# A language-model tower on one core: attention features in 32-row groups, expert loads issued by ScalarE, constants by VectorE, and new orders

## The reference

```python
h = table[x]
h = h + attn0(layernorm(h))        # A: causal linear attention, elu features, 16 heads of 16
h = h + ffn0(layernorm(h))         # A: one 256x256 product, scaled rows
h = h + attn1(layernorm(h))        # B and C: softmax-kernel attention, 64 features a head,
                                   #   its own two layernorms, an FFN 256 -> 1024 -> 256
h = h + moe(layernorm(h))          # C: router, shared expert; then 8 experts, one for each token
# inside attn1, for q and for k:
xp = einsum('bhnd,md->bhnm', x * norm, proj)                        # 16 channels -> 64 features
diag = sum(square(x)) * 0.5 * norm * norm
out = ratio * (exp(xp - diag - stab) + EPS_K)    # stab: max over m for q, over n and m for k
```

## Time and profile before

| | |
|---|---|
| median of 3 runs | 720.42 us (719.12 to 721.68) |
| the profiled execution, its own time | 719.09 us |
| its span, first to last instruction | 717.3 us |
| TensorE busy | 666.2 us (93%) |
| VectorE busy | 488.2 us (68%) |
| ScalarE, GpSimd busy | 282.2 and 272.2 us (39%, 38%) |
| mean granted TensorE clock | 0.979 |

### The profile page before, as it was taken

One profiled execution on the slowest core, in us unless ns is written; L12 is line 12 of the kernel. 1 busy time (PEld: TensorE's weight loads), 2 busy tenths in 40 slices (PEclk: granted clock), 3 DMA queues, 4 the chain that ended last, 5 costly groups with the idle time before them and its releaser, 6 DMA issues.

```text
span 717.3 us, 15031 instructions
## 1 busy us (share of the span) xinstructions
PE 666.2 (93%) x5626; PEld 545.7 (76%) x5627; DVE 488.2 (68%) x1116; ACT 282.2 (39%) x664; POOL 272.2 (38%) x422
## 2 busy tenths in 40 slices
PE   3879899999999999999999999999938699999996
PEld 3667688888898898989888898899937365565654
DVE  1888999999889888888878977867525122323231
ACT  2345456546454462636355263454201032322221
POOL 6244344525426153342504325314201344454542
PEclk9999999999999999999999999999979799999998
DMA  7940000000011010000000000000063411012110
GB/s 266 417 181 9 2 10 8 9 9 9 8 17 16 17 9 16 1 16 9 9 16 1 17 8 9 17 16 8 9 191 117 119 38 48 27 41 66 54 54 11
DMA packets 17296, 34.18 MB, mean 48 GB/s; under 512 B 7617, under 2 KB 12240, under 8 KB 15952
## 3 DMA queue, kind: packets, MB, share of 16 engines
q1 hardware_dynamic: 12640, 24.89, 10.0%
q0 software_dynamic: 4592, 8.41, 4.7%
HBM read 28.74 MB, written 7.29 MB: 50 GB/s over the span
## 4 chain that ended last, share of the span: by engine, by line
PE 79%; DVE 7%; DMA 4%; issue 4%; POOL 3%; ACT 2%; SPq 0%; POOLq 0%; DVEq 0%; ACTq 0%
PE ps L1070 74%; PE ps L1075 2%; DMA x_rows<-send_x 2%; PE ps L1240 2%; DMA sorted_ids<-tokens,slot_u 1%; DVE S_sb L770 1%; DVE stats L711 1%; ACT qkA L687 1%; POOL rstd L412 1%; ACT yTB L677 1%; POOL H L380 1%; POOL preC L471 0%; DMA yA<-x_rows,ids 0%; POOL sorted_ids L483 0%; DVE yA L716 0%
## 5 line engine op out<-in xcount | busy, mean ns | idle before, releaser
L411 POOL TENSOR_TENSOR var_eps<-mv,ln_eps 128x1 f32<-128x1 f32 x112 | 27.7, 248 | 270.3 <-DVE mv L712 269.6
L1070 PE MATMUL ps<-yTC,we 128*128 128x128 f32 x1024 | 125.3, 277 | 0.5 <-DVE yTA L798 0.5
L1070 PEld LDWEIGHTS ps<-yTC,we 128*128 128x128 f32 x1024 | 120.5, 194 | 1.4 <-issue 1.0
L1070 PE MATMUL ps<-we,yTA 128*128 128x256 f32 (+1 forms) x288 | 96.9, 469 | 3.1 <-issue 1.5
L1070 PEld LDWEIGHTS ps<-we,yTA 128*128 128x128 f32 x288 | 54.3, 199 | 27.7 <-issue 22.1
L1070 PE MATMUL ps<-we,yTB 128*128 128x256 f32 (+1 forms) x216 | 71.8, 466 | 0.0
L412 POOL TENSOR_TENSOR rstd<-var_eps,pow_half 128x1 f32<-128x1 f32 x112 | 64.4, 575 | 8.8
L1070 PE MATMUL ps<-we,ffT 128*128 128x256 f32 x256 | 62.0, 385 | 0.0
L1070 PEld LDWEIGHTS ps<-we,yTB 128*128 128x128 f32 x216 | 40.3, 190 | 23.8 <-issue 21.0
L1070 PEld LDWEIGHTS ps<-we,ffT 128*128 128x128 f32 x256 | 46.2, 190 | 8.2 <-issue 3.2
L770 DVE TENSOR_TENSOR S_sb<-ps,causal_sb 128x512 f32<-128x512 f32 x64 | 40.5, 678 | 8.1 <-PE ps L1070 8.1
(11 more groups left out here) (183 smaller groups left out, 1329.1 us busy)
## 6 DMA issues: line engine op xcount, KB each, us to landing
we<-w_experts SPq DMA_DIRECT2D x7, 1536.0 KB, 15.3
we<-w_ff SPq DMA_DIRECT2D x2, 1024.0 KB, 8.4
x_rows<-send_x SPq DMA_DIRECT2D x16, 128.0 KB, 1.7
home_rows<-send_home SPq DMA_DIRECT2D x16, 128.0 KB, 1.7
rows_sb<-rows SPq DMA_DIRECT2D x1, 1664.0 KB, 6.3
we<-w_experts SPq DMA_DIRECT2D x3, 512.0 KB, 3.9
we<-w_qk SPq DMA_DIRECT2D x2, 512.0 KB, 3.7
we<-w_v SPq DMA_DIRECT2D x2, 256.0 KB, 4.0
```

The costliest lines, as they stand in the source:

```text
L411: link(pool.tensor_tensor(var_eps[:, k:k + 1], mv[:, k, 1:2], ln_eps[:], ALU.add))
L1070: return pe.matmul(o, a, b, start=start, stop=stop)
```

## The change

1. **Features in 32-row groups.** `proj_sb` shrinks to blocks of 32 rows (2 heads, 128 columns). One stage `b_kq` replaces `b_k` and `b_q`: 16 matmuls of 128 columns, in turn on the four row groups, each to a PSUM bank of its own. k and q then lie side by side in four banks; ACT copies k out in two instructions, and DVE's `b_qs` reads q in two halves, after ACT's copies (it now waits for `xk_read`).
2. **`a_den`**: eight matmuls of 256 columns in place of 16 of 128.
3. **The late expert loads** stand in ScalarE's table and are issued on its queue. SP keeps `x_out`, `home_out` and the id loads.
4. **The constants** are set by VectorE, before its first statistics.
5. **48 products of a constant** (`ones_sb` by itself, 16 bit) stand first on TensorE.
6. **New orders and lags on all five engines, new PSUM banks** and so new `after(...)` waits.

```diff
-        proj_sb = sb("proj_sb", [P, 4 * M])
+        proj_sb = sb("proj_sb", [P, 2 * M])
...
-            def features(banks, first_chunk):
+            def features(at, first_chunk):
                 for c in range(KD):
-                    for g in range(2):
-                        rows_of = slice(64 * g, 64 * g + 64)
-                        ins = matmul(banks[:, g, c * 4 * M:(c + 1) * 4 * M],
+                    for g in range(4):
+                        rows_of = slice(32 * g, 32 * g + 32)
+                        ins = matmul((xka, xkb)[g // 2][:, g % 2, at + c * P:at + c * P + P],
                                      qkB[rows_of, first_chunk + c, :], proj_sb[rows_of, :], True, True)
...
             def b_rk(t):
-                act.wait_ge(S["xk_psum"], t + 1)
-                after(act, "ctx_psum", t)
-                act.activation(flat(kf[:]), flat(xk), ACT.Copy).then_inc(S["xk_read"], 1)
+                act.wait_ge(S["xkq_psum"], t + 1)
+                for half, banks in enumerate((xka, xkb)):
+                    act.activation(by_bank(kf, half), banks[:, :, D:2 * D], ACT.Copy).then_inc(S["xk_read"], 1)
...
             def b_qs(t):
-                dve.wait_ge(S["xq_psum"], t + 1)
-                link(dve.tensor_reduce(qmax[:, 0, :], x, AX.X, ALU.max))
+                dve.wait_ge(S["xk_read"], t * 2 + 2)
+                dve.tensor_reduce(heads_of(qmax[:, 0, :], 0), halves[0], AX.X, ALU.max).then_inc(S["dve_step"], 1)
+                counted()
+                link(dve.tensor_reduce(heads_of(qmax[:, 0, :], 1), halves[1], AX.X, ALU.max))
                 dve.wait_ge(S["diag_read"], t + 1)
                 link(dve.tensor_tensor(by_group(qmax[:, 1, :]), by_group(qmax[:, 0, :]), diag_of(0), ALU.add))
-                dve.tensor_tensor(qf[:], x, by_head(qmax[:, 1, :], M), ALU.subtract).then_inc(S["qexp_in"], 1)
+                for half in range(2):
+                    dve.tensor_tensor(by_bank4(qf, half), halves[half],
+                                      heads_of(qmax[:, 1, :], half).unsqueeze(3).broadcast_to([P, 2, 4, M]), ALU.subtract
+                                      ).then_inc(S["qexp_in"], 1)
...
+            pe.wait_ge(S["consts_ready"], 1)
+            for _ in range(WARMING):
+                matmul(T0[:, 0:P], ones_sb[:], ones_sb[:], True, True)
...
-                (5, home_out), (0, free_ff), (4, free_ga), (8, ids3), (7, ids1), (2, x_out), (3, ids0), (3, free_up),
-                (2, free_b), (5, free_dn), (7, ids2),
+                (12, ids2), (5, ids1), (4, home_out), (2, ids0), (12, ids3), (0, x_out),
```

More of the change, by code:

```diff
@@ L281, in _ @@
             sp.dma_start(sorted_ids.rearrange("(p n) one -> p (n one)", p=P), nowhere[:]).then_inc(S["ids_cleared"], 16)
[L283 to L287, removed]
+            for e in range(RESIDENT):
+                sp.dma_start(we[:, e * EXPERT:(e + 1) * EXPERT], w_experts[e]).then_inc(S["experts_loaded"], 16)
             def x_out(t):
@@ L666, in c_th, with load_experts, free_b, free_ff @@
                 act.activation(tC[:], ga, ACT.Tanh, scale=0.5).then_inc(S["tanh_gate"], 1)
+            def load_experts(first, last, done):
+                for e in range(first, last):
+                    act.dma_start(we[:, e * EXPERT:(e + 1) * EXPERT], w_experts[e]).then_inc(S[done], 16)
+            def free_b(t):
+                if t == T - 1:
+                    act.wait_ge(S["ffn0_psum"], T)
+                    act.wait_ge(S["out1_psum"], T)
+                    load_experts(RESIDENT, freed_by_b, "experts_loaded")
+            def free_ff(t):
+                if t == T - 1:
+                    act.wait_ge(S["ff2_psum"], 2 * T)
+                    load_experts(freed_by_b, freed_by_ff, "experts_loaded")
+            last = we[:, freed_by_ff * EXPERT:E * EXPERT]
+            def free_part(name, a, b, done):
+                act.wait_ge(S[name], T)
+                act.dma_start(last[:, a:b], w_experts[E - 1][:, a:b]).then_inc(S[done], 16)
+            def free_ga(t):
+                if t == T - 1:
+                    free_part("gate_psum", GATE, UP, "experts_loaded")
+            def free_up(t):
+                if t == T - 1:
+                    free_part("up_psum", UP, DOWN, "experts_loaded")
+            def free_dn(t):
+                if t == T - 1:
+                    free_part("down_psum", DOWN, EXPERT, "last_down_loaded")
             run_steps([
-                (6, b_cx2), (1, a_x), (9, c_tt), (5, b_dgc), (4, a_yT2), (10, c_th), (7, c_ra), (9, c_send),
-                (7, c_rb), (0, a_yT), (5, b_ek), (4, b_yT), (5, b_keps), (1, a_exp), (2, a_rd), (8, c_yT2), (5, b_eq),
-                (6, c_yT), (4, b_x), (4, b_sq), (5, b_rqT), (1, a_par), (4, b_rk),
+                (12, free_up), (1, a_exp), (7, c_rb), (5, b_eq), (0, a_yT), (5, b_rqT), (1, a_par), (4, b_yT),
+                (9, c_tt), (2, a_rd), (9, c_send), (7, free_b), (5, b_ek), (5, b_keps), (4, b_x), (8, free_ff),
+                (4, b_sq), (0, a_x), (10, c_th), (8, c_yT2), (3, a_yT2), (13, free_dn), (6, c_yT), (10, free_ga),
+                (5, b_cx2), (4, b_dgc), (4, b_rk), (6, c_ra),
             ])
@@ L1168, in b_T3 @@
                 pe.wait_ge(S["src3_ready"], t + 1)
+                after(pe, "qT_ready", t)
                 transposed(T3, yB).then_inc(S["src3T_psum"], 1)
@@ L1178, in b_v @@
                 pe.wait_ge(S["src3T_ready"], t + 1)
+                after(pe, "ffa_ready", (t - 2) * 4 + 4)
                 if t + 1 < T:
@@ L1218, in b_kmB, with b_kq @@
                 pe.wait_ge(S["kmax_head"], t + 1)
-                after(pe, "diag_read", t + 1)
                 matmul(kb[:, 0:HEADS], one16[:], km_diag[:], True, True).then_inc(S["kmax_psum"], 1)
-            def b_k(t):
+            def b_kq(t):
                 if t == 0:
```

210 lines of the change are left out of this document (92 added, 118 removed).

## The result

The changed kernel takes 710.58 us (median of 4 runs, 710.16 to 711.62), the one before 720.79 beside it: a ratio of 0.9863, 95% interval 0.9842 to 0.9885. That is 9.9 us less, where 29 were forecast, and outside the range of 681 to 704. The profiled execution took 710.16 us, its span is 708.2.

What follows compares the result with a forecast made beforehand. PE was taken to bound full steps (31.9 us; DVE needs 28.5), PE and DVE abreast the filling, a store wait the draining. Terms -11 - 2.9 - 12 - 3 = -28.9 from 720.42 gave 691 us, range 681 to 704.

Steps and rivals of the forecast that it cites:

- Features, -11: Feature products on PE: 1.1 us less a tile, counted for ten tiles in PE-bound steps; -11 us, bounds -4 and -17.6.
- the first six give nothing: Features of tiles 0 to 5, in steps where DVE has no room: no gain, up to 1.8 us lost.
- The rival of serial weight loads: Weight loads of the features' row groups go one after another, 0.118 us each: 727 us in all; chance 0.05.
- Start, -2.9: POOL's first variance 1.1 us sooner, first 16 products 1.8 us shorter at full clock: -2.9 us, bounds -1 and -3.
- Draining, -12: PE's 10.76 us of idling on a store and 1.2 us of low clock after it go: -12 us, bounds -7 and -12.
- SP's stores no longer stand behind loads: In the draining, stores on SP's queue wait neither behind expert loads nor for `ff2_psum`; reason for the -12 us.
- If the store takes 10 us, 5 are lost again: Draining: tile 14's store leaves together with experts 5 and 6; ACT's `c_send` of tile 15 waits for it.
- Two queues don't part the transfers: Stores and scatter stay slow beside loads on another queue: draining gives 7 us, sorting nothing; 699 us, chance 0.12.
- the store would get its share: Draining: each DMA engine takes turns between queues, so a store beside a load is served and the load loses.
- Sorting, -3: From last counts to first expert product: SP waits for tile rows' table, not scatter, 4.5 us less; -3, bounds 0 and -7.

Runs made afterwards that it cites:

- the compared trace: Trace of the changed kernel with the features alone back in 64-row groups (8 products of 256 columns a tile); 721.45 us, ratio 1.0031 to the kernel before.

## Why the prediction was wrong

**Features, -11: right in size, in part by luck.** 12.1 us measured, give or take 2.3. 1.1 us a tile less of products holds, but 0.27 of it come from standing together; a full step fell by 0.7 to 0.8 us, not by 1.1. Against this, "the first six give nothing" was wrong: the steps of the filling gave 0.8 us each as well. Ten steps of 1.1 and some fifteen of 0.8 come to the same. The rival of serial weight loads is out: 0.031 us a load, under the 0.106 from which it would have decided, while the Trainium skill, TensorE: Matmul & The Clock Gate, "LDWEIGHTS (loading the stationary operand)", has a load cost the same whatever its rows. By that rule 32 loads a tile would be 3.8 us by the full loads' row; they took 0.98.

**Start, -2.9: right up to the draining** (3.1 us at the first copy); in the time it is 1.7 us, give or take 2.4, and so not shown.

**Draining, -12: this step failed.** The prediction wrote that "SP's stores no longer stand behind loads", that tile 14's store leaves "on another queue", and "If the store takes 10 us, 5 are lost again". It took 14.7 us, and in place of one stop of 10.76 us there were two, 7.59 and 7.87, each with low clock behind it. The waits on stores cost 13.2 us in the changed kernel (710.58 to 697.35) and 8.6 before: 4.6 us more (give or take some 4), where 12 less were forecast. Three things were missed. The rival "Two queues don't part the transfers" was put down because a store has whole rows; but loads in whole rows of 12 KB hold up its rows of 1 KB, and loads in pieces of 2 KB hardly do. Its price was counted for one meeting, but expert 4's load, now at 502 us, makes a second. And only `send_x` was followed, not `send_home`, whose wait stands ahead of `c_log` and so of TensorE. The move to ScalarE itself shows no gain: with the loads on SyncE the time is not told from the changed kernel's.

The prediction used the Trainium skill, DMA: Bandwidth & Descriptors, "Queues, rings and completion order", for "the store would get its share". The page has the engines take turns between queues by packets, each a group of several descriptors. The traces agree on turns in part: they are seen in the second meeting, but row for row (108 and 107 of the profile's packets, each a single row), and not in the first. Where they hold, the share in time is small for the queue with the small rows, which I had not worked out.

**Sorting, -3: 0.5 more instead.** The scatter gained 2.5 us (9.97 to 7.42), not 4.5: it was held against a median of 2.3 us that is not the scatters' (7.6), so it still lands after the table of tile rows (545.04 and 544.65). The rest of the way took it back: from the scatter's landing to the first gather it is 0.7 us more (6.1 and 5.5), from there to the first expert product 2.3 us more (8.0 and 5.7). The gathers now stand beside expert 7's loads; the one that the chain waits for took 4.64 us, where the one before took 3.33.

Together: -13.3 us without waits on stores, +4.6 by them, is -8.7, against -9.9 measured between runs on different chips. The 13.3 are 0.5 us less than features and start gave by the times (12.1 + 1.7), less than these differences can tell. They are 4.9 less than by the traces at tile 13's counts (15.3 + 2.9), of which up to 3.5 are the low clock in the filling of the compared trace; where the rest stays was not tried.

## What to carry over

A transfer on another queue is not a transfer out of the way: compare the rows' sizes, and expect a small-row store beside a large-row load to land about when the load lands, or later. Before big loads are moved earlier, give every store that they can meet a second buffer or a source that nobody overwrites, and look for the engine whose next instruction waits for its landing; or cut the load, if an engine has time to issue the pieces. A saved time ahead of such a wait arrives only in part, so measure a term at several marks of the timeline, not by the end alone.

## What the runs showed of the hardware

- A scatter of 128 single numbers takes 7.6 us at the median of the 16 in the kernel before, 7.42 for the last one in the changed kernel with no load beside it, 6.57 beside the last of the 2 KB pieces, and 11.9 to 12.9 beside 4 and 12 KB packets; beside SyncE's dense queue of 2 KB pieces 11.63.
- A store can be out for 5 to 6 us more after the last packet of any queue (512 to 517.61 us in the changed kernel).
- A DMA issue costs ScalarE about 0.4 us alone, but 8.30 us for 12 in a row: 0.69 each, and it stands still meanwhile.
- A 32-row weight load with 128 columns of product behind it costs 0.031 us, less than the 0.045 with 256 columns; a 64-row one costs 23.4 / 256 = 0.091, a full one 0.118.
